# A twelve-layer kernel: the order of work around a recurrent layer that rides inside an FFN pass

## The chip, the core and the metric

The kernel runs on one core of a Trainium2 chip. Five engines work side by side: PE (TensorE, matrix products), DVE (VectorE), ACT (ScalarE), POOL (GpSimd) and SP (SyncE, which only issues transfers here). Each has its own list of instructions, takes them strictly in order, and waits at semaphores for the others. The metric is device time in microseconds; before the change it was 1217.29 us, the median of three runs (1212.4 to 1217.9).

## What is computed

Two sequences of 512 tokens with 256 features pass through twelve layers: four blocks of FFN, token mixing, FFN. The change touches the first block and, of the last one, the preparation of a weight matrix. Cut to that:

```python
def ffn0(x, w_gate, w_up, w_down):                  # 256 -> 1024 -> 256
    return (silu(x @ w_gate.T) * (x @ w_up.T)) @ w_down.T

def rglru(x, W_xy, ig_w, ig_b, ag_w, ag_b, a_param, conv_w, conv_b, W_resid):
    xr, y = split(x @ W_xy.T)                       # 256 features each
    xc = causal_conv1d(xr, conv_w, conv_b)          # 4 taps over time
    gate_x = sigmoid(block_diag(xc, ig_w) + ig_b)
    gate_a = sigmoid(block_diag(xc, ag_w) + ag_b)
    log_a = -8.0 * gate_a * softplus(a_param)
    a = exp(log_a)
    n = xc * gate_x * sqrt(-expm1(2.0 * log_a))
    h = scan(h = a * h + n)                         # over time
    return (gelu(y) * h) @ W_resid.T

def ternary(w):                                     # the last block's FFN weight, 256 x 256
    t = 0.7 * mean(abs(w), axis=-1, keepdims=True)
    return where(w > t, 1, where(w < -t, -1, 0))

x = x + 0.5 * ffn0(layernorm(x))
x = x + rglru(layernorm(x))
x = x + 0.5 * ffn0(layernorm(x))
...                                                 # nine more layers
```

Products are in fp32 precision: each operand is held as a high and a low part (names ending in h and l), and each product is three matmuls (`mm3`, lines 290 to 292).

## The kernel before

**Units.** A unit is one layer for one batch element. Units 0 and 1 are the first FFN for elements 0 and 1, units 2 and 3 the recurrent layer, units 4 and 5 the second FFN. Every engine walks through the units; the code of an engine for a layer is a function such as `pe_ffn`, `act_ffn`, `dve_ffn`. The order inside each of these lists is written out by hand.

**An FFN unit** goes through 8 chunks of 128 hidden features. For chunk j, PE makes gate and up (`gate_up(j)`, 12 matmuls of 512 columns each), ACT the SiLU, DVE the product `ffn_hf`, ACT its high part `ffn_hh` (a rounding copy), DVE the low part `ffn_hl`, and PE the down projection (`down(j)`, 12 matmuls of 256 columns). `chunk(j)` names ACT's or DVE's two steps. SP loads the weights of a chunk into one of two buffers `raw`; POOL splits them into high and low part, gate and up first (lines 522, 525), the down part when the product two chunks back has been used (492, 494). SP loads a chunk when POOL has split the one two back.

**The recurrent layer rides along.** In `RG_OF` unit 1 carries the recurrent layer of element 0 (`r` = 2, `b` = 0), unit 4 that of element 1. Between the chunks PE has the transposes of the normalized x (`pe_T`), the x projection (`pe_rg_x`), the y projection (`pe_rg_y`), the gate products for the two halves of the 256 features (`pe_rg_gates` 0 and 1) and the output projection (`pe_rg_out`). ACT has the convolution's first tap, the high part of its result, the GELU of y, both sigmoids (as Tanh), decay (Exp and Tanh), roots (Sqrt) and the high part of the gated result; DVE has the other taps, the low parts, products, squares, scan, residual and statistics. Projections and gates all write PSUM banks 0 and 1, one after the other; who may write next is told by a semaphore of whoever read last. GELU, SiLU, Exp and Sqrt each want another activation table (Tanh comes with SiLU's and with Exp's), and a change of table is a load on ACT.

**What else is on the lists.** In unit 0, DVE works on sparse positions for a later layer: `d_eq` masks, and in the step behind chunk 7 the rest of a softplus of `a_param` (`dve_softplus_rest`, lines 2685 to 2704) and the places of 2048 entries (2567 to 2574). POOL scatters 16 groups of those entries into a table in HBM, one indirect transfer after the other, each waiting until the one ahead has landed: groups 0 to 5 stand behind the splits of chunks 2 to 7 of unit 1, groups 6 to 9 follow, then comes unit 4's normalization factor (`pool_ln`, line 402); groups 10 to 15 stand in unit 4 in the same way. The four weight blocks of the recurrent layer are split by ACT (`act_rg_weights`) and POOL (`pool_rg_weights`) in unit 0. `dve_ternary` makes the ternary weight: in unit 1 the thresholds, in unit 4 the comparisons. Its matrix `d_q3` is loaded by SP behind the chunks of unit 1 and behind eight stores of zeros (`sp_zero_x`):

```python
            chunks(0)
            chunks(1)
            sp_zero_x(sp)
            sp.dma_start(d_q3[:, :, :], a["weight3"]).then_inc(sem("d_in_q3"), 16)
            chunks(4)
```

`pe_warm` is 12 matmuls whose result nobody reads. They stand ahead of the last down projection of units 1 and 4 and behind the transposes that follow it.

## Time and profile before

| | |
|---|---|
| runs | 1217.29 us median (1212.4, 1217.29, 1217.9) |
| profiled execution | 1215.54 us, its span 1213.3 us |
| PE, DVE, ACT, POOL busy | 91%, 68%, 50%, 45% of the span |
| granted TensorE clock, mean | 0.976 of full speed |
| units 0, 1, 4 | unit 1 begins at 71.96, unit 4 at 139.75, unit 5 at 207.52 us |

In a row of the trace the first number is the start in us from the start of the span, the second the duration in us, then engine, line, operation, written and read tiles, shape; in brackets the idle time of that engine just before, and the engine and line whose work ended it. A line can be that of a helper: lines 290 to 292 are all products, 728 and 732 ACT's two steps of a chunk, 776 and 783 DVE's. Rows of one kind in a row are merged (x4).

### The profile page before, as it was taken

The page shows a single profiled execution, that of the slowest core. Times are in us where ns is not written, and L with a number is a line of the kernel's source. Part 1 is how long each engine was busy: PE and PEld are TensorE (multiplying, and loading weights), DVE is VectorE, ACT ScalarE, POOL GpSimd, SP SyncE. Part 2 cuts the span into 40 slices and gives each one's busy share as a digit, 9 for nine tenths or more (in the row PEclk, how much of TensorE's full clock was granted, in tenths as well). Part 3 has the DMA queues.
Part 4 walks back from the last instruction along what each step waited for, and adds up shares of the span by engine and source line. Part 5 has one row for each costly group of instructions (what it writes and reads, how often), then busy time and mean ns, then how long its engine had stood idle before and what let it go on. Part 6 is the DMA issues. An engine that isn't in the chain of part 4 may idle for free.

```text
span 1213.3 us, 22107 instructions
## 1 busy us (share of the span) xinstructions
PE 1106.9 (91%) x6833; PEld 934.7 (77%) x6833; DVE 827.2 (68%) x2280; ACT 605.2 (50%) x1422; POOL 544.0 (45%) x662
## 2 busy tenths in 40 slices
PE   5988796999899999998989999998899998999997
PEld 4867685777667779966767777996799997899995
DVE  4866657687988865658867876566766665665666
ACT  3436463521112345557747856555455554555552
POOL 6647573751446452235424426324353442444431
PEclk9999997999899999999999999999999999999999
DMA  7215123130004023422102163343011110110101
GB/s 247 89 53 205 29 65 109 57 122 20 1 8 182 1 93 117 136 69 60 34 17 45 43 238 102 117 131 105 28 43 35 43 35 27 37 42 26 52 0 35
DMA packets 48181, 87.81 MB, mean 72 GB/s; under 512 B 9505, under 2 KB 28321, under 8 KB 47521
## 3 DMA queue, kind: packets, MB, share of 16 engines
q1 hardware_dynamic: 41536, 72.98, 19.1%
q0 software_dynamic: 3968, 8.85, 2.5%
q10 hardware_dynamic: 2592, 4.92, 1.2%
q8 instruction: 45, 0.74, 0.3%
q14 instruction: 40, 0.32, 0.1%
HBM read 61.23 MB, written 19.20 MB: 66 GB/s over the span
## 4 chain that ended last, share of the span: by engine, by line
PE 63%; DVE 21%; ACT 8%; issue 4%; DMA 2%; POOL 2%; SPq 1%; DVEq 0%; POOLq 0%; ACTq 0%
PE ps L290 19%; PE ps L292 17%; PE ps L291 17%; DVE a_ptl L1918 4%; PE ps L1894 3%; DVE a_p L1853 2%; ACT a_pth L1910 2%; ACT a_p L1861 2%; PE ps L460 1%; DVE x L1607 1%; PE ps L941 1%; DMA rg_wf<-in_rglru 1%; DVE xl L454 1%; DVE x L1122 1%; PE ps L960 1%
## 5 line engine op out<-in xcount | busy, mean ns | idle before, releaser
L1879 POOL TENSOR_SCALAR a_p<-a_p,small 128x128 f32<-128x128 f32 (+3 forms) x256 | 132.0, 532 | 219.9 <-DVE small L1870 219.8
L1861 ACT ACTIVATE a_p<-a_p,small 128x128 f32<-128x128 f32 (+3 forms) x256 | 141.6, 554 | 77.3 <-DVE small L1853 75.1
L1918 DVE TENSOR_TENSOR a_ptl<-ps,a_pth 128x384 fp32r<-128x384 f32 (+1 forms) x192 | 106.6, 596 | 61.7 <-ACT a_pth L1910 61.5
L290 PE MATMUL ps<-xh,wh 128*128 128x512 f32 x304 | 125.9, 414 | 9.2 <-DVE xl L454 8.1
L291 PE MATMUL ps<-xl,wh 128*128 128x512 f32 x304 | 122.7, 404 | 0.0
L292 PE MATMUL ps<-xh,wl 128*128 128x512 f32 x304 | 122.7, 404 | 0.0
L1910 ACT ACTIVATE a_pth<-ps 128x384 fp32r<-128x384 f32 (+1 forms) x192 | 90.3, 524 | 59.3 <-PE ps L1894 59.2
L1853 DVE CUSTOM_DVE_ANT_0 a_p<-ps,maskrow 128x128 f32<-128x128 f32 (+3 forms) x256 | 111.7, 483 | 4.8 <-PE ps L292 2.1
L402 POOL TENSOR_TENSOR rstd<-veps,nhalf 128x4 f32<-128x4 f32 x24 | 25.9, 1079 | 174.9 <-DVE veps L346 174.9
L494 POOL TENSOR_TENSOR wl<-raw,wh 128x256 fp32r<-128x256 f32 (+1 forms) x64 | 86.2, 1347 | 5.3
L1894 PE MATMUL ps<-ident,a_p 128*128 128x128 f32 x640 | 83.7, 277 | 5.2 <-DVE a_ptl L1918 2.2
L290 PE MATMUL ps<-m_a,xh 128*128 x240 | 83.2, 347 | 5.3 <-DVE xl L1232 2.7
L492 POOL TENSOR_SCALAR wh<-raw 128x256 fp32r<-128x256 f32 (+1 forms) x64 | 46.8, 731 | 80.2 <-PE ps L292 80.1
L1894 PEld LDWEIGHTS ps<-ident,a_p 128*128 128x128 f32 x640 | 71.6, 143 | 8.4 <-DVE a_ptl L1918 2.6
L290 PEld LDWEIGHTS ps<-xh,wh 128*128 128x128 f32 x304 | 59.1, 194 | 24.3 <-DVE xl L454 10.2
L291 PE MATMUL ps<-m_b,xh 128*128 x240 | 72.7, 303 | 0.0
L292 PE MATMUL ps<-m_a,xl 128*128 x240 | 72.5, 302 | 0.0
L292 PEld LDWEIGHTS ps<-xh,wl 128*128 128x128 f32 x304 | 58.7, 193 | 14.5
L1607 DVE SCALAR_TENSOR_TENSOR x<-ps,small,x 128x256 f32<-128x256 f32 x128 | 61.8, 483 | 9.9 <-PE ps L292 3.6
L291 PEld LDWEIGHTS ps<-xl,wh 128*128 128x128 f32 x304 | 59.1, 194 | 11.3
L290 PE MATMUL ps<-drh,xh 128*128 (+2 forms) x160 | 61.7, 385 | 4.0 <-DVE x L1607 4.0
L291 PE MATMUL ps<-drl,xh 128*128 (+2 forms) x160 | 60.3, 377 | 0.0
(366 smaller groups left out, 3352.8 us busy)
## 6 DMA issues: line engine op xcount, KB each, us to landing
raw<-in_w SPq DMA_DIRECT2D x32, 384.0 KB, 3.2
raw<-in_qk SPq DMA_DIRECT2D x16, 512.0 KB, 3.5
raw<-moe_x SPq DMA_DIRECT2D x60, 128.0 KB, 2.3
moe_y<-m_y SPq DMA_DIRECT2D x60, 128.0 KB
m_raw<-in_ex SPq DMA_DIRECT2D x8, 608.0 KB, 7.5
m_a<-in_ex SPq DMA_DIRECT2D x8, 608.0 KB, 5.5
raw<-in_v SPq DMA_DIRECT2D x16, 256.0 KB
moe_x<-drh SPq DMA_DIRECT2D x8, 480.0 KB, 6.1
```

The source lines that it names most:

```text
L290: pe.matmul(o, l[0], r[0], start=start, stop=False, skip_group_check=True)
L291: pe.matmul(o, l[0], r[1], start=False, stop=False, skip_group_check=True)
L292: return pe.matmul(o, l[1], r[0], start=False, stop=stop, skip_group_check=True)
L492: g.tensor_scalar(oh, raw[:, p, at:n], 1.0, 1.0, ALU.mult, ALU.mult).then_inc(sem("w_hi"), 1)
L494: g.tensor_tensor(ol, raw[:, p, at:n], f32(oh), ALU.subtract).then_inc(sem("w_split"), 1)
L1607: v.scalar_tensor_tensor(out=xt, in0=ps[:, 2 + t, e * D:(e + 1) * D], scalar=w_moe1[:, t, 2 * k + e:2 * k + e + 1], in1=xt, op0=ALU.mult, ...
L1853: v.tensor_tensor_reduce(p[:, par, P_AT[i]:P_AT[i + 1]], ps[:, bank, at:at + KEYS[i]], maskrow[:, T - KEYS[i]:T], 1.0, -NEG, ALU.add, ALU.min,
L1861: s.activation(p[:, par, P_AT[i]:P_AT[i + 1]], p[:, par, P_AT[i]:P_AT[i + 1]], ACT.Exp, bias=h_nmx[:, par, i:i + 1], scale=scale, accum_ou ...
L1879: g.tensor_scalar(pp, pp, h_inv[:, par, i:i + 1], 1.0, ALU.mult, ALU.mult).then_inc(sem("at_norm"), 1)
L1894: last = pe.transpose(ps[:, banks[f], at:at + P], p[:, par, P_AT[i] + kb * P:P_AT[i] + (kb + 1) * P], ident[:, :])
L1910: s.activation(dst, ps[:, bank, 0:cols], func, **how).then_inc(sem("at_fhi"), 1)
L1918: ins = v.tensor_tensor(dst, ps[:, bank, 0:cols], f32(hi), ALU.subtract)
```

## The change

PE, ACT and DVE get another order in units 1 and 4; waits are set to match it.

- PE: the gate products move ahead of the y projection and one chunk earlier, the y projection behind `down(4)`, the output projection ahead of `down(5)`.
- ACT: the sigmoids move one chunk earlier, the GELU between roots and gated result, and chunk 5 behind the gated result. Three chunks follow it then, where there were two.
- DVE: the same for its steps; chunk 5 stands ahead of the residual, chunk 6 behind the statistics. Softplus' rest moves from unit 0 to unit 1, behind the low part of the recurrent layer's x; the five place operations (`dve_places`) to the start of unit 1; `dve_ternary` from the end of units 1 and 4 to the place between the first gate product and chunk 4.
- Waits for `const_rgp`, which softplus' rest sets, move from the x projection and the padding to the sigmoids.
- In unit 0 the four weight blocks are copied by ACT behind chunks 0 and 1 (before: two ahead of unit 0, two behind chunk 0) and subtracted by POOL one behind each of chunks 2 to 5 (before: two ahead of chunk 2, then one behind chunks 2 and 3).

```diff
                 gate_up(3)
-                pe_rg_y(pe, r)
+                pe_rg_gates(pe, r, 0)
                 down(2)
                 gate_up(4)
                 down(3)
-                pe_rg_gates(pe, r, 0)
+                pe_rg_gates(pe, r, 1)
                 gate_up(5)
                 down(4)
-                pe_rg_gates(pe, r, 1)
+                pe_rg_y(pe, r)
                 gate_up(6)
+                pe_rg_out(pe, r)
                 down(5)
                 gate_up(7)
-                pe_rg_out(pe, r)
                 down(6)
...
                 act_rg_conv_hi(s, r, 1)
-                act_rg_gelu(s, r)
+                act_rg_sigmoids(s, r, 0)
                 chunk(4)
-                act_rg_sigmoids(s, r, 0)
-                chunk(5)
                 act_rg_sigmoids(s, r, 1)
                 act_rg_decay(s, r)
                 act_rg_roots(s, r)
+                act_rg_gelu(s, r)
                 act_rg_gated_hi(s, r)
+                chunk(5)
                 chunk(6)
                 chunk(7)
...
                     dve_combined(v)
+                    dve_places(v)
                 chunk(0)
                 chunk(1)
                 dve_rg_pad(v, r)
                 dve_T(v, r)
+                if u == 1:
+                    dve_softplus_rest(v)
                 dve_rg_conv(v, r, 0)
                 chunk(2)
                 dve_rg_conv_lo(v, r, 0)
                 dve_rg_conv(v, r, 1)
                 chunk(3)
                 dve_rg_conv_lo(v, r, 1)
+                dve_rg_gate_input(v, r, 0)
+                dve_ternary(v, u)
                 chunk(4)
-                dve_rg_gate_input(v, r, 0)
-                chunk(5)
                 dve_rg_gate_input(v, r, 1)
                 dve_rg_square(v, r, 0)
                 dve_rg_square(v, r, 1)
                 dve_rg_scan(v, r)
                 dve_rg_gated_lo(v, r)
-                chunk(6)
+                chunk(5)
                 dve_residual(v, r, 1.0, [("rg_out", 2 * (r - 2) + 1), ("rg_out", 2 * (r - 2) + 2)], rg_o)
                 dve_stats(v, nxt)
+                chunk(6)
                 chunk(7)
                 dve_residual(v, u, 0.5, ready)
-                dve_ternary(v, u)
                 dve_T(v, nxt)
...
-                    pe.wait_ge(sem("rg_gelu"), DC * b + k + 1)
+                    pe.wait_ge(sem("rg_tap"), DC * b + k + 1)
...
-                pe.wait_ge(sem("rg_tap"), DC * b + c + 1)
+                pe.wait_ge(sem("rg_sigm"), 4 * b + 2 + c + 1)
...
-            if u == 0 and j == 0:
-                act_rg_weights(s, 2)
-                act_rg_weights(s, 3)
+            if u == 0 and j <= 1:
+                act_rg_weights(s, 2 * j)
+                act_rg_weights(s, 2 * j + 1)
...
-            pool_rg_weights(g, 0)
-            pool_rg_weights(g, 1)
             for i in range(1, CH0 // 2):
                 for p in range(2):
                     pool_chunks(g, 0, i, p)
-                    if i == 1:
-                        pool_rg_weights(g, 2 + p)
+                    if i <= 2:
+                        pool_rg_weights(g, 2 * i + p - 2)
```

`dve_places` holds the five operations that stood at lines 2567 to 2574, with the same waits between them.

Three places as they stand on the engines. DVE at the end of unit 0, before (`small` is softplus' data, `d_col` to `d_desti` the places, `xl` the low part of the next unit's x, L477 the residual):

```order
L2703 TENSOR_SCALAR rgp<-rgp 128x2x2
L2704 TENSOR_SCALAR rgp<-small 128x2
L2567 TENSOR_SCALAR d_col<-d_col 128x16
L2568 TENSOR_SCALAR d_col<-d_col 128x16
L2570 TENSOR_TENSOR d_col<-d_col 128x16
L2572 CAST d_small<-d_col 128x16
L2574 CAST d_desti<-d_small 128x16
L454 TENSOR_TENSOR xl<-ps,xh 128x512 x2
L477 SCALAR_TENSOR_TENSOR x<-ps,x 128x256 x4
```

And after, from the last chunk of unit 0 to the first product of unit 1:

```order
L783 TENSOR_TENSOR ffn_hl<-ffn_hf,ffn_hh 128x512
L454 TENSOR_TENSOR xl<-ps,xh 128x512 x2
L477 SCALAR_TENSOR_TENSOR x<-ps,x 128x256 x4
L336 BN_STATS stats<-x 128x6 x4
L342 BN_AGGR mv<-stats 128x2 x4
L345 TENSOR_SCALAR negm<-mv 128x4
L346 TENSOR_SCALAR veps<-mv 128x4
L2536 COPY d_work<-ps 128x128
L2539 TENSOR_TENSOR d_work<-d_work,ps 128x128 x2
L2522 TENSOR_SCALAR d_col<-d_col 128x16
L2523 TENSOR_SCALAR d_col<-d_col 128x16
```

The low part of x follows the last chunk directly, and the places stand ahead of unit 1's first product.

DVE in unit 1 from chunk 3 on, before (`rg_cl` is the low part of the convolution, `rg_xc<-rg_xp,rg_xc` the gate product):

```order
L776 TENSOR_TENSOR ffn_hf<-ffn_s,ps 128x512
L783 TENSOR_TENSOR ffn_hl<-ffn_hf,ffn_hh 128x512
L1505 TENSOR_TENSOR rg_cl<-rg_xc,rg_ch 128x512
L776 TENSOR_TENSOR ffn_hf<-ffn_s,ps 128x512
L783 TENSOR_TENSOR ffn_hl<-ffn_hf,ffn_hh 128x512
L1511 SCALAR_TENSOR_TENSOR rg_xc<-rg_xp,rg_xc 128x512
```

And after (L2616 to L2622 are the ternary thresholds, `d_q` the loaded matrix):

```order
L776 TENSOR_TENSOR ffn_hf<-ffn_s,ps 128x512
L783 TENSOR_TENSOR ffn_hl<-ffn_hf,ffn_hh 128x512
L1510 TENSOR_TENSOR rg_cl<-rg_xc,rg_ch 128x512
L1516 SCALAR_TENSOR_TENSOR rg_xc<-rg_xp,rg_xc 128x512
L2616 TENSOR_SCALAR d_q3n<-d_q 128x512
L2618 TENSOR_TENSOR d_q3t<-d_q,d_q3n 128x512
L2620 TENSOR_REDUCE d_small<-d_q3t 128x2
L2622 TENSOR_SCALAR d_small<-d_small 128x2
L776 TENSOR_TENSOR ffn_hf<-ffn_s,ps 128x512
L783 TENSOR_TENSOR ffn_hl<-ffn_hf,ffn_hh 128x512
L1516 SCALAR_TENSOR_TENSOR rg_xc<-rg_xp,rg_xc 128x512
```

The first gate product and the thresholds stand ahead of chunk 4 now.

ACT behind the roots of unit 1, before (L1478 is the high part of the gated result, L728 with L732 a chunk, L358 the next unit's normalization):

```order
L1472 ACT_TABLE_LOAD
L1472 ACTIVATE rg_ga<-rg_ga 128x512 x2
L1478 ACTIVATE rg_ch<-rg_gy 128x512 x2
L728 ACT_TABLE_LOAD
L728 ACTIVATE ffn_s<-ps 128x512
L732 ACTIVATE ffn_hh<-ffn_hf 128x512
L728 ACTIVATE ffn_s<-ps 128x512
L732 ACTIVATE ffn_hh<-ffn_hf 128x512
L358 ACTIVATE xn<-x,nmr,rstd 128x256 x4
```

And after (L1449 is the GELU):

```order
L1477 ACT_TABLE_LOAD
L1477 ACTIVATE rg_ga<-rg_ga 128x512 x2
L1449 ACT_TABLE_LOAD
L1449 ACTIVATE rg_gy<-ps 128x512 x2
L1483 ACTIVATE rg_ch<-rg_gy 128x512 x2
L728 ACT_TABLE_LOAD
L728 ACTIVATE ffn_s<-ps 128x512
L732 ACTIVATE ffn_hh<-ffn_hf 128x512
L728 ACTIVATE ffn_s<-ps 128x512
L732 ACTIVATE ffn_hh<-ffn_hf 128x512
L728 ACTIVATE ffn_s<-ps 128x512
L732 ACTIVATE ffn_hh<-ffn_hf 128x512
```

The GELU with its table stands behind the roots, and three chunks stand behind the gated result.

## Rows read from the trace of the kernel before

**Rows 1.** The chain that ended last, as shares of the span by engine:

```profile
PE 63%; DVE 21%; ACT 8%; issue 4%; DMA 2%; POOL 2%; SPq 1%; DVEq 0%; POOLq 0%; ACTq 0%
```

**Rows 2.** PE's timeline, units 0 to 5, at the places named:

```profile
23.14 0.39 PE L290 MATMUL ps<-wh,ffn_hh 128*128 128x256 f32 x1 [1.03 <-DVE ffn_hl L783]
...
71.96 0.51 PE L290 MATMUL ps<-xh,wh 128*128 128x512 f32 x1 [2.82 <-DVE xl L454]
...
83.99 0.50 PE L290 MATMUL ps<-xh,rch 128*128 128x512 f32 x1 [1.26 <-DVE xl L454]
...
122.97 0.58 PE L290 MATMUL ps<-rch,rg_ch 128*128 128x256 f32 x1 [6.37 <-DVE rg_cl L1544]
...
132.70 0.39 PE L290 MATMUL ps<-wh,ffn_hh 128*128 128x256 f32 x1 [0.81 <-DVE ffn_hl L783]
...
135.09 1.06 PE L426 MATMUL ps<-ident,xn 128*128 128x128 f32 x8 [0.69 <-issue]
...
139.75 0.50 PE L290 MATMUL ps<-xh,wh 128*128 128x512 f32 x1 [1.00 <-DVE xl L454]
...
150.22 0.49 PE L290 MATMUL ps<-xh,rch 128*128 128x512 f32 x1 [1.42 <-DVE xl L454]
...
189.19 0.58 PE L290 MATMUL ps<-rch,rg_ch 128*128 128x256 f32 x1 [6.37 <-DVE rg_cl L1544]
...
207.52 0.50 PE L290 MATMUL ps<-xh,wh 128*128 128x512 f32 x1 [2.62 <-DVE xl L454]
```

**Rows 3.** DVE's timeline at the end of unit 0 and in unit 1:

```profile
65.78 0.16 DVE L2685 TENSOR_SCALAR small<-small 128x2 f32<-128x2 f32 x1
...
68.75 0.16 DVE L2567 TENSOR_SCALAR d_col<-d_col 128x16 int32<-128x16 int32 x1
...
70.63 1.28 DVE L454 TENSOR_TENSOR xl<-ps,xh 128x512 fp32r<-128x512 f32 x2
...
76.67 0.69 DVE L776 TENSOR_TENSOR ffn_hf<-ffn_s,ps 128x512 f32<-128x512 f32 x1 [0.61 <-PE ps L292]
...
87.16 2.46 DVE L1499 SCALAR_TENSOR_TENSOR rg_xc<-rg_xp,rgp,rg_xc 128x512 f32<-128x512 f32 x3 [3.23 <-ACT rg_xc L1438]
...
98.02 0.69 DVE L1505 TENSOR_TENSOR rg_cl<-rg_xc,rg_ch 128x512 fp32r<-128x512 f32 x1
```

**Rows 4.** SP's timeline in unit 1, the eight stores and the matrix load:

```profile
104.96 6.90 SPq L2409 DMA_DIRECT2D moe_x<-drh  x8
111.90 1.26 SPq L2725 DMA_DIRECT2D d_q<-in_weight  x1
```

**Rows 5.** The view of tile d_q: its load, from issue to landing:

```profile
DMA to landing us min/median/max: 6.9/6.9/6.9
```

**Rows 6.** Windows of DVE's old ternary work (window, length, DVE busy, clock, DMA share, GB/s):

```profile
135.10:138.50 3.40, 3.30 (x6) 1.00 0.33 89
201.90:206.26 4.36, 4.33 (x7) 1.00 0.86 357
```

**Rows 7.** ACT's timeline in unit 1, first second-half sigmoid and second root:

```profile
108.83 0.69 ACT L1455 ACTIVATE rg_xp<-ps,rgp 128x512 f32<-128x512 f32 x1 [0.69 <-PE ps L292]
...
116.73 0.63 ACT L1472 ACTIVATE rg_ga<-rg_ga 128x512 f32<-128x512 f32 x1 [0.32 <-DVE rg_ga L1521]
```

**Rows 8.** POOL's timeline, scatters 6, 8 and 9 and unit 4's normalization:

```profile
121.81 1.33 POOL L2419 DMA_INDIRECT delta_table<-d_work,d_desti  x1 [2.79 <-DMA delta_table<-d_work,d_desti]
...
128.20 0.96 POOL L2419 DMA_INDIRECT delta_table<-d_work,d_desti  x1 [2.71 <-DMA delta_table<-d_work,d_desti]
130.56 0.96 POOL L2419 DMA_INDIRECT delta_table<-d_work,d_desti  x1 [1.40 <-DMA delta_table<-d_work,d_desti]
131.54 1.05 POOL L402 TENSOR_TENSOR rstd<-veps,nhalf 128x4 f32<-128x4 f32 x1
```

**Rows 9.** Windows: length, PE, PEld, DVE, ACT, POOL busy, granted clock, DMA, GB/s:

```profile
123.00:127.80 4.80, 4.80 (x25) 4.80 (x26) 2.04 (x4) 2.20 (x4) 1.10 (x2) 0.58 0.03 5
207.50:214.80 7.30, 7.28 (x25) 5.75 (x26) 3.72 (x12) 2.74 (x3) 3.13 (x4) 0.77 0.11 42
```

More of the change, by code:

```diff
@@ L1420, in pe_rg_out @@
             b = r - 2
+            pe.wait_ge(sem("rg_gelu"), DC * (b + 1))
             pe.wait_ge(sem("rg_glo"), DC * (b + 1))
@@ L1432, in act_rg_x @@
             b = r - 2
-            s.wait_ge(sem("const_rgp"), 2)
+            s.wait_ge(sem("const_in"), 16 * CONSTS)
             s.wait_ge(sem("rg_pad"), b + 1)
@@ L1453, in act_rg_sigmoids @@
             b = r - 2
+            s.wait_ge(sem("const_rgp"), 2)
             s.wait_ge(sem("rg_gates"), 4 * b + 2 * c + 1)
@@ L1484, in dve_rg_pad @@
             b = r - 2
-            v.wait_ge(sem("const_rgp"), 2)
+            v.wait_ge(sem("const_in"), 16 * CONSTS)
             if b == 0:
@@ L2506, in dve_equal, with dve_places, step, settled @@
                     .then_inc(sem("d_eqs"), 1)
+        def dve_places(v):
+            def step(ins):
+                ins.then_inc(sem("d_step"), 1)
+                d_steps[0] += 1
+            def settled():
+                v.wait_ge(sem("d_step"), d_steps[0])
+            step(v.tensor_scalar(d_col[:, 1, :], d_col[:, 0, :], D - 1, 8, ALU.bitwise_and, ALU.logical_shift_left))
+            step(v.tensor_scalar(d_col[:, 2, :], d_col[:, 0, :], 8, None, ALU.logical_shift_right))
+            settled()
+            step(v.tensor_tensor(d_col[:, 3, :], d_col[:, 1, :], d_col[:, 2, :], ALU.bitwise_or))
+            settled()
+            step(v.tensor_copy(d_dest, d_col[:, 3, :]))
+            settled()
+            v.tensor_copy(d_desti[:, :], d_dest).then_inc(sem("d_dest"), 1)
         def dve_combined(v):
@@ L2564, in dve_delta @@
                 v.tensor_scalar(sp_u, sp_y, 1.0, None, ALU.add).then_inc(sem("sp_u"), 1)
-            if u == 0 and j == 7:
-                dve_softplus_rest(v)
-                then(v.tensor_scalar(d_col[:, 1, :], d_col[:, 0, :], D - 1, 8, ALU.bitwise_and, ALU.logical_shift_left))
-                then(v.tensor_scalar(d_col[:, 2, :], d_col[:, 0, :], 8, None, ALU.logical_shift_right))
-                settled()
-                then(v.tensor_tensor(d_col[:, 3, :], d_col[:, 1, :], d_col[:, 2, :], ALU.bitwise_or))
-                settled()
-                then(v.tensor_copy(d_dest, d_col[:, 3, :]))
-                settled()
-                v.tensor_copy(d_desti[:, :], d_dest).then_inc(sem("d_dest"), 1)
             if u == 5 and j == 5:
@@ L2833, in _ @@
             act_T(s, 0)
-            act_rg_weights(s, 0)
-            act_rg_weights(s, 1)
             for u in range(stop):
```

## The prediction

> **What bounds the kernel now.** The chain that ended last comes first: 63% of it is TensorE (PE), 21% DVE [rows 1]. So TensorE's time counts, and an edit pays or costs only where TensorE waits. The change lies in units 0, 1 and 4: three FFN passes, of which unit 1 carries the recurrent layer of batch element 0 and unit 4 that of element 1. TensorE's rows there show where it waits, all for DVE: 2.82 us ahead of unit 1, 6.37 us ahead of each recurrent output projection, 1.00 us ahead of unit 4, 2.62 us ahead of unit 5 [rows 2]. Below, a time in a recurrent unit counts from that unit's x projection, 83.99 in unit 1 and 150.22 in unit 4. From there to the next unit's first matmul it was 139.75 - 83.99 = 55.8 us and 207.52 - 150.22 = 57.3 us; the output projection began at 39.0 in both (122.97, 189.19).
>
> From 83.99 to 122.97 - 6.37 = 116.60 TensorE never pauses and issues 108 matmuls of 512 columns and 60 of 256, worth 138 of 512: 32.61 / 138 = 0.236 us each. So a gate/up pair (12) is 2.83 us, a down projection 1.42, the two gates of one half 1.42, the y projection 2.83, the 12 warm-up matmuls 2.8.
>
> **Start (term A: -0.5).** Two recurrent weight copies leave ScalarE ahead of its first SiLU. TensorE's 1.03 us wait at 23.14 [rows 2] is the most that this gives back. Their two POOL subtracts don't vanish: one stands now behind each of four weight chunks, so later chunks are split later, and TensorE follows those. I take half, -0.5, between -1.0 and +0.6.
>
> **Softplus' rest and the places (term B: -1.3).** From 65.78 to 70.63 DVE worked on both while the transposed x waited [rows 3]. That x needs only ScalarE's copy, so DVE's subtract moves up some 2.7 us and nearly all of the 2.82 us wait goes. But the next link is DVE's product at 76.67, which had waited 0.61 us for TensorE, and the five place operations (68.75 to 70.63, 1.9 us) stand right ahead of it now: -2.7 + 1.9 - 0.6 = -1.4, taken as -1.3 since TensorE pauses longer there. Bounds: -2.3 (places take 1 us when POOL is still), -0.5 (TensorE comes back at its low clock). Softplus' rest (65.78 to 68.75, 3.0 us) goes behind the subtract of the recurrent layer's x, where DVE sat idle 3.23 us for ScalarE [rows 3]; it costs nothing as long as that cover holds, and up to 3.0 if it doesn't.
>
> **Unit 1 (term C: +25.3).** Two things get queued behind something late.
>
> First, the ternary work. Its first DVE step waits for the 256 KB weight matrix, whose load stays where it was in SP's queue: behind unit 1's last chunk and eight zero stores. It was issued at 111.90 [rows 4] and took 6.9 us to land [rows 5]: at 118.8, or 34.8 in unit time. The old place of the work, 135.1, was later than that; the new one is not. SP gets past unit 1's last chunk (stores from 104.96) when POOL has split chunk 5, and that follows down(3), which the new order reaches without the y projection and with one pair of gates ahead: 2.83 - 1.42 = 1.4 us earlier. So the matrix lands at 33.4. DVE is there after the second convolution half (98.02 + 0.69 - 83.99 = 14.7 [rows 3]) and one gate product of that size: at 15.4. It waits 18 us, and behind the waiting instruction stand chunk(4), the second gate product, squares and scan. ScalarE (second-half sigmoids behind chunk(4)) waits for DVE, TensorE stops at down(4), POOL at chunk 6. The work took 3.4 us with POOL beside it [rows 6]; with POOL stopped I take 2.6. DVE is free at 36.0.
>
> From there the path is the old one, entered one chunk earlier: chunk(4)'s product and copy, 1.3 us, then second-half sigmoids to output projection as before, 122.97 - 108.83 = 14.1 us, less 0.3 for the wait ahead of the second root [rows 7]. The GELU now between root and gated copy has room under DVE's scan, since ScalarE had nothing there. Output projection at 36.0 + 15.1 = 51.0, where it was 39.0: **+12.0**. The table load that each unit saves earns nothing, ScalarE being the one that waits.
>
> Second, what follows the projection. Three chunks stand behind it instead of two. A down projection whose product is queued behind residual and statistics started 132.70 - 122.97 = 9.7 us after it [rows 2]; that is down(6) now, then come warm-up, down(7), transposes: 9.7 + 1.4 + 2.8 + 1.4 = 15.3 us. With transposes (1.0) and warm-up the next unit could start 19.1 us after the projection (before: 16.8). But POOL is later still. Its split of chunk 7 needs down(5), which follows the projection now (4.8 + 1.4 us), so it ends at +7.8. Behind it in POOL's queue stand scatters 5 to 9, each waiting for the one ahead to land, and only then unit 4's normalization. Undisturbed steps took (130.56 - 121.81) / 3 = 2.92 us, the last issue 1.0 [rows 8]: normalization at 7.8 + 4 x 2.92 + 1.0 = +20.5, transposes 135.09 - 131.54 = 3.55 us later, at +24.0. Before, the scatters ran beside the scan and were done in time. TensorE has paused 7 us by then. After its 6.37 us pause it ran 4.8 us at a granted clock of 0.58 [rows 9], a mix of 1.2 and 2.4 GHz; so transposes and warm-up, 3.8 us at full clock, take 4.8 + (3.8 - 0.58 x 4.8) = 5.8, about 6. Next unit at +30.0, not +16.8: **+13.3**. Sum +25.3. Bounds: ternary 1.9 to 3.4; a scatter step 2.36 to 3.67, the shortest and longest undisturbed one (-2.2 to +3.0); transposes and warm-up 3.8 to 7.6.
>
> The Trainium skill, "DMA: Bandwidth & Descriptors", section Anatomy of one DMA, fits a POOL-queue DMA with about 2.0 us plus bytes over 436 GB/s. By that (an estimate) a scatter of 4 KB would step at 2.0 and not 2.92, and the sum would be 3.7 us less. The rows decide here.
>
> **Unit 4 (term D: -5.7).** Nothing is loaded here. Ternary's second half is arithmetic, 4.3 us with POOL beside it [rows 6]; I take 3.3 (1.9 to 4.3). From 15.4 that frees DVE at 18.7; + 15.1 puts the output projection at 33.9, not 39.0: -5.1. Behind it 19.1 us, not 207.52 - 189.19 = 18.3: +0.8. POOL has one scatter there, so it is in time. Ternary no longer stands ahead of unit 5's x: the 2.62 us wait goes, and the low clock behind it: the 24 matmuls that follow took 7.3 us at a granted 0.77 [rows 9], at 0.236 they take 5.7, and I count -1.4.
>
> **Sum.** -0.5 - 1.3 + 25.3 - 5.7 = +17.8. The profiled execution took 1215.5 us (span 1213.3), 0.14% under the median of the runs, 1217.29. 1215.5 + 17.8 = 1233.3, say **1233**.
>
> **Rivals.**
> (1) Faster: the transfers are hidden. With the matrix there at 15.4, 18 us sooner, and scatters under 0.7 us apart, DVE is free at 18.0, the projection starts at 33.0, the next unit at 52.1, not 55.8: -3.7, in all -11.2: 1204.3. For it: unit 4 will look so. Against: nothing moved in SP's queue [rows 4]. 0.04.
> (2) Matrix in time, scatters not: 33.0 + 30.0 = 63.0, +7.2, in all -0.3: 1215.2. 0.03.
> (3) Matrix late, scatters hidden: 51.0 + 19.1 = 70.1, +14.3, in all +6.8: 1222.3. For it: before, they ended in time for the transposes [rows 2, 8]. Against: five landings don't fit into 3 us. 0.08.
>
> **Chances.** The forecast has 0.85. Faster by over 0.5% (6 us, about what a measurement of this kernel can tell from no change): rival 1, 0.04. Within: rival 2 and half of rival 3, 0.07. Slower: 0.89. The bounds of the terms, seldom all at one end, give 1225 to 1240; the rivals, 0.15, stay outside.
>
> **What would show it.** Right: in unit 1 a first ternary row on DVE behind some 18 us of idle time that the weight load ends; TensorE idle some 17 us ahead of down(4); five scatters between unit 1's last split and unit 4's normalization on POOL, and TensorE's transposes behind that; no wait over 1 us ahead of units 1 and 5; unit 4's output projection near 34. Wrong: a ternary row within 1 us of the gate product (rivals 1, 2), or transposes some 15 us behind the projection (rival 3).

## The result and the profile after

The changed kernel took 1235.91 us (median of 4 runs, 1234.34 to 1238.6) against 1217.6 us (4 runs, 1212.4 to 1223.2): ratio 1.0158, 95% interval 1.0127 to 1.019. That is 18.3 us slower. The prediction was 1233.0, with a range of 1225 to 1240. The profiled execution took 1236.6 us, its span 1234.1.

The chain that ended last looks as it did [rows 1]; shares over the whole span don't show a change of 1.6%:

```profile
PE 62%; DVE 21%; ACT 8%; issue 5%; POOL 2%; DMA 1%; SPq 1%; DVEq 0%; POOLq 0%; ACTq 0%
```

PE's timeline of the changed kernel, at the places that answer to [rows 2] (start, length, operation, and in brackets the idle time ahead and what ended it):

```profile
24.85 0.50 PE L290 MATMUL ps<-xh,wh 128*128 128x512 f32 x1 [0.83 <-POOL wl L525]
...
67.51 0.50 PE L290 MATMUL ps<-xh,wh 128*128 128x512 f32 x1
...
80.05 0.68 PE L290 MATMUL ps<-xh,rch 128*128 128x512 f32 x1
...
117.96 0.58 PE L290 MATMUL ps<-wh,ffn_hh 128*128 128x256 f32 x1 [16.03 <-DVE ffn_hl L783]
...
131.96 0.55 PE L290 MATMUL ps<-rch,rg_ch 128*128 128x256 f32 x1 [5.16 <-DVE rg_cl L1549]
...
154.81 1.94 PE L426 MATMUL ps<-ident,xn 128*128 128x128 f32 x8 [7.80 <-issue]
...
160.15 0.58 PE L290 MATMUL ps<-xh,wh 128*128 128x512 f32 x1
...
206.85 0.55 PE L290 MATMUL ps<-rch,rg_ch 128*128 128x256 f32 x1 [6.47 <-DVE rg_cl L1549]
...
225.14 0.58 PE L290 MATMUL ps<-xh,wh 128*128 128x512 f32 x1
```

The waits ahead of units 1, 4 and 5 are gone, and two new ones stand in unit 1: 16.03 us ahead of down(4), and 7.80 us ahead of unit 4's transposes. The second is put down to "issue", PE's own queue; POOL's and ACT's rows below show whom it waited for.

DVE's timeline of the changed kernel shows the first one, from the gate product to chunk 4:

```profile
96.55 1.10 DVE L1516 SCALAR_TENSOR_TENSOR rg_xc<-rg_xp,rg_xc 128x512 f32<-128x512 f32 x1
113.81 0.43 DVE L2616 TENSOR_SCALAR d_q3n<-d_q 128x512 f32<-128x512 f32 x1 [16.16 <-DMA d_q<-in_weight]
...
115.83 0.69 DVE L776 TENSOR_TENSOR ffn_hf<-ffn_s,ps 128x512 f32<-128x512 f32 x1
```

And SP's timeline says why the matrix came then: the load still stands behind the zero stores, as in [rows 4]:

```profile
100.72 8.19 SPq L2414 DMA_DIRECT2D moe_x<-drh  x8
108.95 1.19 SPq L2738 DMA_DIRECT2D d_q<-in_weight  x1
```

It landed 4.8 us after its issue, by the view of tile d_q (6.9 before [rows 5]):

```profile
DMA to landing us min/median/max: 4.8/4.8/4.8
```

POOL's timeline of the changed kernel shows the second wait: the down split of chunk 7, five scatters, unit 4's normalization (to compare with [rows 8]).

```profile
137.95 0.41 POOL L492 TENSOR_SCALAR wh<-raw 128x256 fp32r<-128x256 f32 x1 [11.51 <-PE ps L292]
...
139.33 1.06 POOL L2424 DMA_INDIRECT delta_table<-d_work,d_desti  x1 [0.16 <-issue]
143.23 0.96 POOL L2424 DMA_INDIRECT delta_table<-d_work,d_desti  x1 [2.84 <-DMA delta_table<-d_work,d_desti]
145.58 0.96 POOL L2424 DMA_INDIRECT delta_table<-d_work,d_desti  x1 [1.39 <-DMA delta_table<-d_work,d_desti]
147.93 0.96 POOL L2424 DMA_INDIRECT delta_table<-d_work,d_desti  x1 [1.40 <-DMA delta_table<-d_work,d_desti]
150.28 0.96 POOL L2424 DMA_INDIRECT delta_table<-d_work,d_desti  x1 [1.39 <-DMA delta_table<-d_work,d_desti]
151.27 1.05 POOL L402 TENSOR_TENSOR rstd<-veps,nhalf 128x4 f32<-128x4 f32 x1
```

ACT's timeline: the normalization of x that the transposes need, idle until POOL was done:

```profile
152.64 2.07 ACT L358 ACTIVATE xn<-x,nmr,rstd 128x256 f32<-128x256 f32 x4 [10.13 <-POOL nmr L406]
```

All runs can be laid side by side by the starts of four stages on PE, as above. x1 and x4 are the recurrent x projections of units 1 and 4, R1 and R4 the output projections, U4 and U5 the first matmuls of the next units; "rest" is from U5 to the end of the span. Times in us, one profile each:

| kernel | x1 | x1 to R1 | R1 to U4 | U4 to x4 | x4 to R4 | R4 to U5 | rest |
|---|---|---|---|---|---|---|---|
| before | 83.99 | 38.98 | 16.78 | 10.47 | 38.97 | 18.33 | 1005.8 |
| before again (e10) | 82.56 | 38.96 | 17.21 | 10.48 | 39.01 | 17.48 | 1007.4 |
| after | 80.05 | 51.91 | 28.19 | 10.56 | 36.14 | 18.29 | 1009.0 |
| after again (e6) | 81.22 | 51.76 | 30.12 | 10.58 | 36.18 | 18.57 | 1009.2 |
| e1 early load | 80.61 | 36.86 | 29.46 | 10.56 | 36.16 | 18.45 | 1009.3 |
| e2 ternary at ends | 82.94 | 34.60 | 28.16 | 10.56 | 34.46 | 20.19 | 1006.0 |
| e3 scatters in gap | 81.25 | 51.74 | 19.56 | 10.57 | 36.14 | 18.93 | 1008.6 |
| e4 e1 and e3 | 79.93 | 36.65 | 18.51 | 10.58 | 36.18 | 18.08 | 1006.1 |
| e5 e3, ternary behind chunk 7 | 81.23 | 34.44 | 19.80 | 10.56 | 34.47 | 20.19 | 1008.1 |
| e7 before, ternary moved alone | 82.88 | 52.71 | 15.82 | 10.55 | 40.02 | 15.16 | 1008.6 |
| e8 before, new start alone | 79.64 | 39.29 | 17.04 | 10.48 | 39.01 | 17.87 | 1011.9 |
| e9 e3, ternary in unit 4's holes | 80.49 | 34.43 | 19.62 | 10.56 | 34.47 | 18.08 | 1006.2 |

### The profile page after: what moved, and what is told of

It is laid out like the page before. It is cut to its first block, busy times and chain, and to the rows that moved or that the text cites. A ratio compares the mean times of both kernels' runs of the same rounds, so it can differ in the third digit from the quotient of the medians.

```text
span 1234.1 us, 22111 instructions
## 1 busy us (share of the span) xinstructions
PE 1113.2 (90%) x6833; PEld 940.0 (76%) x6833; DVE 827.4 (67%) x2280; ACT 602.4 (49%) x1420; POOL 542.8 (44%) x662
## 4 chain that ended last, share of the span: by engine, by line
PE 62%; DVE 21%; ACT 8%; issue 5%; POOL 2%; DMA 1%; SPq 1%; DVEq 0%; POOLq 0%; ACTq 0%
PE ps L290 18%; PE ps L291 16%; PE ps L292 16%; DVE a_ptl L1923 4%; PE ps L1899 3%; PE ps L460 2%; DVE a_p L1858 2%; ACT a_pth L1915 2%; ACT a_p L1866 1%; DVE x L1612 1%; PE ps L426 1%; PE ps L944 1%; DVE stats L336 1%; DVE x L1125 1%; PE ps L963 1%
## 5 line engine op out<-in xcount | busy, mean ns | idle before, releaser
L732 ACT ACTIVATE ffn_hh<-ffn_hf 128x512 fp32r<-128x512 f32 x32 | 20.2, 632 | 89.8 <-DVE ffn_hf L776 89.8
```

## The experiments

The theory, from the prediction: two transfers cost some 25 us, the weight load that DVE waits for in order and the scatters that POOL runs through ahead of unit 4's normalization; the rest of the change gains some 8 us. The main rival: the new order, three chunks behind the tail, is itself what costs. The first four kernels tell these apart, each against runs of the kernel before.

**e1: the load earlier in SP's queue.**

```diff
             chunks(0)
+            sp.dma_start(d_q3[:, :, :], a["weight3"]).then_inc(sem("d_in_q3"), 16)
             chunks(1)
             sp_zero_x(sp)
-            sp.dma_start(d_q3[:, :, :], a["weight3"]).then_inc(sem("d_in_q3"), 16)
```

> The changed kernel with one line moved: SP issues the load of the weight matrix ahead of unit 1's weight chunks instead of behind them and the eight stores of zeros. Theory (DVE's in-order wait of 16.16 us for this load sets the output projection of unit 1): the wait is gone, the first ternary operation follows the gate product at once, the output projection comes about 36 us after the x projection as in unit 4 (now 51.9), and with the scatters still ahead of unit 4's normalization (next unit 28.2 us behind the output projection) the time falls by 15 to 16 us, to about 1220. Rival (the three chunks behind the tail cost the time, the wait only fills a gap that PE would have anyway): under 3 us, about 1234. Rival (something else on the path is nearly as late, a scatter or a weight split): 5 to 10 us.

Measured: 1221.49 us, ratio to the kernel before 1.0028 (1.001 to 1.0047). DVE's timeline of e1, same place as above:

```profile
96.81 1.10 DVE L1516 SCALAR_TENSOR_TENSOR rg_xc<-rg_xp,rg_xc 128x512 f32<-128x512 f32 x1
97.83 0.84 DVE L2616 TENSOR_SCALAR d_q3n<-d_q 128x512 f32<-128x512 f32 x1
```

No wait is left, x1 to R1 falls from 51.9 to 36.9, and the time by 14.4 us. R1 to U4 stays at 29.5: the second cost doesn't depend on the first.

**e2: the ternary work back at the ends of both units.**

```diff
                 dve_rg_gate_input(v, r, 0)
-                dve_ternary(v, u)
                 chunk(4)
...
                 dve_residual(v, u, 0.5, ready)
+                dve_ternary(v, u)
                 dve_T(v, nxt)
```

> The changed kernel with the ternary work alone put back to the ends of units 1 and 4, where the kernel before has it; the load stays where it is. Theory: no 16 us wait, and DVE's tail starts without the ternary work, so unit 1's output projection comes 32 to 34 us after its x projection (now 51.9) and unit 4's 32 to 34 (now 36.1); the scatters keep unit 4's start 28 us behind the output projection; the ternary operations at the ends cost 0 to 3 us in unit 4 and nothing in unit 1, where the scatters are later. About 1216 (1213 to 1220). Rival (the new order of chunks, not the load, makes unit 1 late): 1230 or more.

Measured: 1219.58 us, ratio 1.0009 (0.9988 to 1.003): the upper end of what was expected. Both output projections came as expected (34.6, 34.5). What fell short of 1216 was x1, 82.94 in this profile, and R4 to U5, 20.2 and not 18.3. At the end of unit 4 the ternary work is not free: PE waits for DVE there again, 0.88 us. Another 0.7 us of it stand ahead of down(6), which came 10.1 us behind R4 and 9.4 in after, with the ternary work in neither stretch.

**e3: the scatters in POOL's idle gap.** Groups 5 to 9 are issued inside chunk 7 of unit 1, where POOL stood idle for 11.51 us until down(5) let the down split go.

```diff
-        def pool_chunks(g, u, i, p):
+        def pool_chunks(g, u, i, p, mid=()):
...
+                if mid:
+                    pool_scatter(g, mid)
                 if positive(ring - 1):
                     g.wait_ge(sem("w_used"), ring - 1)
...
-                    pool_chunks(g, 1, i, p)
-                    pool_scatter(g, [2 * i + p - 2])
-            pool_scatter(g, range(6, 10))
+                    last = (i, p) == (CH0 // 2 - 1, 1)
+                    pool_chunks(g, 1, i, p, range(5, 10) if last else ())
+                    if not last:
+                        pool_scatter(g, [2 * i + p - 2])
```

> The changed kernel with scatter groups 5 to 9 issued on POOL inside unit 1, between the gate and up split and the down split of chunk 7, where POOL stood idle for 11.51 us, instead of behind chunk 7 and ahead of unit 4's normalization; the load stays late. Theory (the scatters alone hold unit 4's start 28.2 us behind the output projection): unit 4 starts 18 to 19 us behind the output projection as unit 5 does, the time falls by 9 to 10 us, to about 1226.5; the 16 us wait stays. Rival (the transposes or the last down products bind as well): 0 to 4 us, 1232 to 1236.

Measured: 1225.83 us, ratio 1.0068 (1.0047 to 1.0089), 10.1 us under the changed kernel. POOL's timeline of e3, the last scatter and the normalization:

```profile
137.79 0.96 POOL L2426 DMA_INDIRECT delta_table<-d_work,d_desti  x1 [1.40 <-DMA delta_table<-d_work,d_desti]
140.33 0.40 POOL L492 TENSOR_SCALAR wh<-raw 128x256 fp32r<-128x256 f32 x1 [1.59 <-PE ps L292]
...
141.80 1.05 POOL L402 TENSOR_TENSOR rstd<-veps,nhalf 128x4 f32<-128x4 f32 x1 [0.24 <-DVE veps L346]
```

The last scatter is issued at 137.79, POOL then waits for PE and DVE again, and the transposes follow down(7) without a pause. R1 to U4 is 19.6, the wait for the load stays at 16.00 us.

**e4: both edits**, e1's line and e3's, in the changed kernel.

> Both edits: the load ahead of unit 1's chunks and scatter groups 5 to 9 in POOL's gap before the down split of chunk 7. Theory: the two costs add, so about 1236 - 15.8 - 9.7 = 1210.5, under the kernel before by 5 to 9 us, since the earlier start of unit 1's x projection (3.9 us) and unit 4's shorter tail (4.4 us) are left. Rival (the order itself costs in both units): 1217 or more. Rival (the gap on POOL is filled by the scatters once the wait for the load is gone, and the down split of chunk 7 comes late): 1213 to 1216.

Measured: 1209.45 us, ratio 0.9938 (0.9915 to 0.9961). The two gains add: 14.4 + 10.1 = 24.5 us one by one, 26.5 together. So the two transfers are the cost, and the new order without them is faster than the kernel before. The rival falls.

**e7: does the wait for the load need the new order?** The ternary work alone is moved, in the kernel before.

```diff
                 dve_rg_gate_input(v, r, 0)
+                dve_ternary(v, u)
                 chunk(5)
...
                 dve_residual(v, u, 0.5, ready)
-                dve_ternary(v, u)
                 dve_T(v, nxt)
```

> The kernel before with one edit: the ternary work of units 1 and 4 behind the first gate product of the recurrent layer instead of at the ends; the order of the gates, the y projection and the chunks as before. Theory: the wait for the load costs the old order too. DVE comes to the ternary work at about 105.4, the load lands at 118.8 or a little earlier, DVE is free at about 120.8, and chunk 5, the second gate product and the tail behind it bring the output projection to 133 to 138 instead of 122.97; but chunk 7's split no longer waits for the output projection, so the scatters end before unit 4's normalization needs POOL and cost nothing: +10 to +15 us from unit 1, 0 to +3 from the ternary half in unit 4, about 1231 (1227 to 1236). Rival (the wait needs the new order of chunks to cost): under +5 us, 1222 or less. Rival (the scatters bind here too): 1240 or more.

Measured: 1227.2 us, ratio 1.0089 (1.0056 to 1.0121). DVE's, POOL's and PE's timelines of e7:

```profile
118.68 0.43 DVE L2603 TENSOR_SCALAR d_q3n<-d_q 128x512 f32<-128x512 f32 x1 [14.38 <-DMA d_q<-in_weight]
```

```profile
139.00 0.96 POOL L2419 DMA_INDIRECT delta_table<-d_work,d_desti  x1 [1.67 <-DMA delta_table<-d_work,d_desti]
144.01 1.05 POOL L402 TENSOR_TENSOR rstd<-veps,nhalf 128x4 f32<-128x4 f32 x1 [4.06 <-DVE veps L346]
```

```profile
135.59 0.58 PE L290 MATMUL ps<-rch,rg_ch 128*128 128x256 f32 x1 [6.27 <-DVE rg_cl L1544]
```

In the old order the wait costs 13.7 us up to R1 (52.7 for 39.0) and the scatters nothing: POOL was through and stood idle 4.06 us for DVE's statistics. The first cost belongs to the moved ternary work, the second to the moved chunks. Unit 4 and its end gave back 1.7 us (55.2 from x4 to U5, 56.9 on average before), where 0 to +3 was expected, and R1 to U4 another 1.2 (15.8 for 17.0). Hence 1227, at the low end of the expected range, and not 1231.

**e8 and e10: the start alone, and the kernel before once more.** e8 is the kernel before with only the new places of the weight splits, of softplus' rest, of the five place operations and of the constants' wait; its core:

```diff
-            if u == 0 and j == 0:
-                act_rg_weights(s, 2)
-                act_rg_weights(s, 3)
+            if u == 0 and j <= 1:
+                act_rg_weights(s, 2 * j)
+                act_rg_weights(s, 2 * j + 1)
...
                     dve_combined(v)
+                    dve_places(v)
...
                 dve_T(v, r)
+                if u == 1:
+                    dve_softplus_rest(v)
```

> The kernel before with only the start of the change: the weight splits spread over unit 0, softplus' rest and the places in unit 1, the constants' wait moved; the recurrent units' order as before and the ternary work at their ends. The prediction put this at -1.8 us (1215.5); the x projections of the five traces of the changed code so far stand at 79.9 to 82.9 against 83.99, so -1 to -4, mean -3.0. Theory now: 1214.5 (1213.5 to 1216.5). Rival (the gain is an accident of the one profile before, whose unit 0 was slow): 1217 to 1218, no difference.

> The kernel before once more, for a second profile. Theory (the start edits are worth about 3 us): unit 1's x projection at 82.5 to 84 again (83.99 before, 82.88 in e7 with the same unit 0; 79.6 to 82.9 in the seven traces with the new start), and from unit 5's start to the end 1006 to 1012 us, as the other traces have it. Rival (the start differs by chance alone): an x projection under 81.5.

Measured: e8 1217.15 us, ratio 0.998 (0.9957 to 1.0004); e10 1215.19 us, a single run. By its time e8 lies in the rival's range and outside the theory's. e10 came as its theory had it, with x1 at 82.56 and a rest of 1007.4. The marks and the times say different things. Nine profiles with the new start have x1 at 79.6 to 82.9, mean 80.8; three with the old one at 82.6, 82.9 and 84.0, mean 83.1. That is 2.3 us, with one overlap (e2). In e8's times 1.1 us is left, and its interval holds zero. So the start's gain is read off the marks and not shown by the times: the rest of the program, the same code in all twelve, took 1005.8 to 1011.9, a scatter wider than the effect, and the 1011.9 are those of e8.

**e6: the changed kernel once more.**

> The changed kernel itself once more, for a second profile and more times. By marks in the traces the first profile started unit 5 17.6 us later than the kernel before and made 1.5 us of that good at once, yet ended 20.8 us later, with stretches of half clock around 358 and 1044 us that the profile before has shorter or not at all. Theory (these stretches scatter between executions): the difference at unit 5's start is again 16 to 18 us, and other or no half-clock stretches follow; time 1233 to 1238. Rival (the change shifts later work into half clock for good): the same stretches stand at the same places, and the difference at the end is 20 us or more again.

Measured: 1237.37 us, ratio 1.0157 (1.0124 to 1.019). U5 stood at 225.14 and 228.43 in the two profiles of after, at 207.52 and 205.70 in those of before: 20.2 us apart on average, over the 16 to 18 that the theory had. The rest was 1009.0 and 1009.2, 1 us over the mean of all twelve profiles. The stretch of half clock near the end came again, and the two spans end 24.3 us apart (1237.6 and 1213.3), as the rival has it. But the kernel before has the stretch too, in e10. Windows of after and of e10 (window, length, PE, PEld, DVE, ACT, POOL busy, granted clock, DMA share, GB/s):

```profile
1033.00:1039.00 6.00, 5.23 (x21) 4.54 (x20) 1.71 (x3) 1.58 (x3) 4.22 (x3) 0.50 0.33 97
```

```profile
1010.00:1017.00 7.00, 6.23 (x28) 5.54 (x28) 1.71 (x3) 1.58 (x3) 4.97 (x4) 0.54 0.25 84
```

e3, which keeps the 16 us wait, has no such stretch (granted clock 1.00 from 990 to 1050). Of the twelve profiles seven have it, four with the new order (after, e6, e1, e5) and three with the old (e10, e7, e8). Their rest is 1009.1 us on average, that of the other five 1006.5. So it comes and goes with either kernel, goes with some 2.5 us, and isn't what the change costs.

**e5 and e9: a better place for the ternary work.** With the scatters in the gap, the ternary work costs 1.7 to 2.2 us of each tail (x to R 36.2 to 36.7 with it, 34.5 without). e5 puts both halves behind chunk 7, ahead of the last residual.

```diff
                 dve_rg_gate_input(v, r, 0)
-                dve_ternary(v, u)
                 chunk(4)
...
                 chunk(7)
+                dve_ternary(v, u)
                 dve_residual(v, u, 0.5, ready)
```

> The changed kernel with scatter groups 5 to 9 in POOL's gap (as in e3) and the ternary work of both units behind chunk 7 and ahead of the last residual, where DVE stood idle for 2.8 to 3.1 us waiting for PE; the load stays in its late place. Theory: the load has landed by then, DVE's tail starts without the ternary work, so output projections come 34.5 us behind the x projections in both units (e2 showed 34.6 and 34.5; e4 has 36.7 and 36.2), next units 18.5 us behind them: 3.7 us under e4, about 1205.7 (1203 to 1208). Rival (the ternary work, 2.0 and 2.3 to 4.3 us there, spills over the hole and delays the residual or the transposed operand): 1208 to 1211.

Measured: 1208.36 us, ratio 0.9922 (0.9895 to 0.9949). The time lies in the rival's range, just over the theory's. The tails came as expected, the ends didn't: R1 to U4 19.8 and R4 to U5 20.2, against 18.5 and 18.1 in e4. About half of that is PE's clock: from output projection to the next down projection, the same matmuls, it took 5.26 us in both units of e5, 4.44 and 4.24 in e4. Windows of unit 1 in e5 and in e4 (granted clock 0.50 and 0.62):

```profile
115.67:120.93 5.26, 5.26 (x24) 5.26 (x25) 2.04 (x4) 2.15 (x4) 1.56 (x2) 0.50 0.09 32
```

```profile
116.58:121.02 4.44, 4.44 (x25) 4.44 (x26) 2.05 (x4) 2.14 (x4) 1.64 (x2) 0.62 0.03 6
```

In unit 4 the edit doesn't set this: e9, whose output projection there follows the same idle time (5.42 us), took 4.24 us at 0.65. In unit 1 ACT's timeline of e5 shows POOL late again, since the projection comes 2 us earlier and the five scatters don't:

```profile
129.98 2.08 ACT L358 ACTIVATE xn<-x,nmr,rstd 128x256 f32<-128x256 f32 x4 [2.82 <-POOL nmr L406]
```

The ternary work itself fits its hole in unit 1, where DVE still waits 0.43 us for PE behind it. In unit 4 it spills over, as the rival has it: PE waits 0.35 us for DVE ahead of U5. e9 moves both halves into unit 4, where e4 showed DVE idle for 2.12 us ahead of chunk 0 and for 3.22 us ahead of the convolution.

```diff
                     dve_places(v)
+                else:
+                    dve_ternary(v, 1)
                 chunk(0)
...
                     dve_softplus_rest(v)
+                else:
+                    dve_ternary(v, 4)
                 dve_rg_conv(v, r, 0)
```

> The changed kernel with scatter groups 5 to 9 in POOL's gap (as in e3), and both ternary halves in unit 4, in two holes that the traces of e4 show on DVE: the first half (2.0 us) ahead of chunk 0, where DVE stood idle for 2.12 us, the second (2.3 us) behind the transposed operand and ahead of the convolution, where it stood idle for 3.22 us. Theory: both tails start without ternary work (output projections 34.6 us behind the x projections), nothing stands at the ends (next units 18.5 and 18.1 us behind them), and unit 4's x projection stays 10.6 us behind its start: x projection of unit 1 to the start of unit 5 in 116.2 us (before 123.5, e4 120.0, e5 119.5), about 1205.5 (1203 to 1208). Rival (the first half is later than the hole allows and moves chunk 0 of unit 4, as it spilled over in e5): 118 to 120 us on that stretch, 1207 to 1210.

Measured: 1207.07 us, ratio 0.9922 (0.99 to 0.9944). DVE's timeline of e9, both halves and what follows each:

```profile
135.59 0.42 DVE L2621 TENSOR_SCALAR d_q3n<-d_q 128x512 f32<-128x512 f32 x1
...
137.78 0.69 DVE L778 TENSOR_TENSOR ffn_hf<-ffn_s,ps 128x512 f32<-128x512 f32 x1
...
144.96 0.34 DVE L2631 TENSOR_SCALAR d_q<-d_q,d_small 128x256 f32<-128x256 f32 x1
...
147.15 1.74 DVE L2634 TENSOR_TENSOR d_q3t<-d_q,d_q3n 128x512 f32<-128x512 f32 x1
148.81 2.31 DVE L1509 SCALAR_TENSOR_TENSOR rg_xc<-rg_xp,rgp,rg_xc 128x512 f32<-128x512 f32 x3
```

U4 to x4 stays at 10.56, so the first half is hidden whole, and x4 to R4 at 34.47, so the second is too. x1 to U5 is 117.2 us, expected 116.2, before 123.5. R1 to U4, 19.6 and not 18.5, is what fell short. About half is again the low clock behind the output projection (5.26 us at 0.50 to 4.44 at 0.62, of which 0.6 is left at down(6), after a shorter wait for DVE). The other half stands ahead of the transposes, where ACT waits 2.63 us for POOL as in e5. e4, e5 and e9 are all faster than both kernels; their intervals overlap, and e9 has the lowest median.

## Why the prediction was right

It foresaw the sign, the size, both mechanisms and their place. Step by step, with the averages of the two profiles of each kernel where there are two:

**Start and places (terms A and B), -1.8 predicted, -2.3 by the marks of all twelve profiles, -2.6 by these four.** In the first pair of profiles it looked like -3.94; more profiles brought it back. The 1.03 us wait at the first down projection (0.59 in e10) went. The 0.83 us that PE waits for POOL's split at 24.85, which is what the prediction halved the term for, stand in the first profile of after alone: in e6 and e8, with the same start, PE goes on there without a pause. The places took 1.2 us and not 1.9 (71.52 to 72.76), near the bound for a still POOL, but in e10 they took 1.4 at their old place. The cover for softplus' rest held, with 0.51 us of idle time left ahead of the convolution. How the gain splits between A and B no run shows.

**Unit 1 (term C), +25.3 predicted, +25.0 measured.** x1 to U4 was 80.10 and 81.88, before 55.76 and 56.17. The output projection came 12.9 us later, predicted 12.0, and what follows it took 12.2 us more, predicted 13.3. That these two misses cancel is luck. Inside the term:

- The matrix landed at 33.7 us of unit time, predicted 33.4. Two errors cancelled: the issue came at 28.9, not 26.5, behind stores that began 1.1 us later and took 8.19 us and not 6.90, and the landing took 4.8, not 6.9. From the first store to the landing it was 13.0 us, and 13.8 before.
- DVE came to the ternary work at 17.6 and not 15.4 (96.55 + 1.10 - 80.05). The wait was 16.2 instead of 18. This cost nothing, the load being last.
- The ternary work took 2.0 us, not 2.6; DVE was free at 35.8, predicted 36.0.
- From there to the output projection it took 16.1 us, not 15.1 (14.9 in e7), so R1 is 51.9 and not 51.0. The rows name the operation. After and e7 run the same two products behind the second root:

```profile
124.56 2.44 DVE L1533 TENSOR_TENSOR rg_xc<-rg_xc,rg_ga 128x512 f32<-128x512 f32 x2 [0.69 <-ACT rg_ga L1477]
```

```profile
129.42 1.29 DVE L1528 TENSOR_TENSOR rg_xc<-rg_xc,rg_ga 128x512 f32<-128x512 f32 x2 [0.69 <-ACT rg_ga L1472]
```

In after, POOL's timeline has chunk 7's split at that time; in e7 POOL was between two scatters:

```profile
124.83 1.62 POOL L525 TENSOR_TENSOR wl<-raw,wh 128x512 fp32r<-128x512 f32 x1
```

The pair ends at 127.00, 0.55 us behind POOL's 126.45, about the time of one of the two products. POOL's operation took 1.62 us here, and 1.27 at 153.26, when DVE stood idle. The Trainium skill ("SBUF — State Buffer", section SBUF: two separate sides) says that a VectorE operation with two SBUF inputs and a GpSimd operation that reads SBUF exclude each other for a whole instruction. These rows agree: the pair took 1.15 us more in after than in e7.

- Normalization at R1 + 19.3, predicted 20.5: the steps between undisturbed scatters were 2.35 us, the lower bound, not 2.92. The first step, 3.90 us, took some of that back. It is the step from scatter 5 to 6, which the sum had left out: 4.36 us in the profile before (from 117.45 to 121.81). The fit of the Trainium skill ("DMA: Bandwidth & Descriptors", section Anatomy of one DMA) that the prediction weighed gives about 2.0 us, an estimate, for such a transfer. The measured 2.35 differs from it, and decides. It lies between that figure and the row that the sum took, and 2.36 stood already in [rows 8], between the last two scatters.
- Transposes to U4 took 5.34 us, predicted 6. e4, where PE doesn't pause ahead of them, has 3.27. The granted clock in these windows, of after and of e4:

```profile
154.81:160.15 5.34, 5.34 (x20) 3.06 (x21) 3.21 (x12) 1.20 (x2) 3.81 (x7) 0.61 0.29 82
```

```profile
131.82:135.09 3.27, 3.27 (x22) 1.96 (x21) 2.96 (x8) 1.08 (x2) 2.08 (x3) 1.00 0.36 120
```

So 2.1 us of the second cost is the low clock after the pause, as the prediction counted it. e1, e2 and e6, which pause there too (7.7 to 7.9 us), ran the same stretch at a granted clock of 0.53 to 0.62. The prediction's +30.0 compares with 28.2 and 30.1.

**Unit 4 (term D), -5.7 predicted, -2.3 measured** (x4 to U5: 54.43 and 54.75, before 57.30 and 56.49). This is the term that was mis-sized, by 3.4 us, in two steps. The first is worth 2.0 us: up to U5 the prediction had -4.3, the other -1.4 lie behind it. x4 to R4 was 36.1, predicted 33.9: the ternary half took 4.3 us (186.57 to 190.82), the upper bound, with POOL splitting weights beside it, and not 3.3; DVE came to it 0.5 us later, and the tail behind it was longer by 0.9. DVE's timeline of after, the half's first and last operation and the next chunk:

```profile
186.57 0.70 DVE L2626 TENSOR_SCALAR d_q<-d_q,d_small 128x256 f32<-128x256 f32 x1
...
189.71 1.19 DVE L2629 TENSOR_TENSOR d_q3t<-d_q,d_q3n 128x512 f32<-128x512 f32 x1
190.82 0.67 DVE L776 TENSOR_TENSOR ffn_hf<-ffn_s,ps 128x512 f32<-128x512 f32 x1
```

e2 and e9 show what the half itself costs there: R4 at 34.5 without it. The second step is the -1.4 us for unit 5's low clock, which was no property of the kernel before. Windows of e10, the second profile of before, and of after, the same 24 matmuls at unit 5's start:

```profile
205.70:211.53 5.83, 5.83 (x24) 4.42 (x25) 3.69 (x12) 2.55 (x3) 3.11 (x4) 1.00 0.13 50
```

```profile
225.14:231.06 5.92, 5.92 (x27) 4.48 (x25) 3.03 (x10) 2.56 (x3) 3.14 (x4) 1.00 0.15 56
```

Where the profile that the prediction read has 0.77 [rows 9], e10 has full clock, behind a wait of 2.25 us (2.62 in [rows 2]).

**Sum.** -2.6 + 25.0 + 0.1 (U4 to x4) - 2.3 = +20.2 up to U5, by the four profiles; the prediction, without its 1.4 us behind U5, had +19.2. The medians differ by 18.3 and, beside e6, by 19.2, but the spans of the four profiled executions by 22.7, 2.5 of it in the rest. So the stages and the medians agree to some 2 to 4 us and no better. The prediction put its +17.8 on a profiled execution that lay 2 us under the median of the four runs of before. So the hit to within 3 us is partly luck: in the two halves of term C, in term D, which the start's gain made up in part, and in executions that scatter by as much. The middle, two waits of some 12 us each that are made by two different parts of the change, was measured part by part. Rivals 1 and 3, the cases without one or both transfers, are kernels now: e4 came to 1209.5 (rival 1: 1204.3), e3, with the load late and the scatters hidden, to 1225.8 (rival 3: 1222.3), e1, with the load in time and the scatters bound, to 1221.5 (rival 2: 1215.2). Each is 3.5 to 6.3 us over the prediction's figure. Term D's 3.4 and the 2 us by which the profile before lay under its median make about that much, though no run takes the two apart.

## What to carry to other kernels

Before work moves to an earlier place on an in-order engine, look up when its inputs land: the transfer keeps its place in the other queue, and everything behind the work waits with it. Before a group of chunks moves behind a long tail, look at what stands behind the last chunk on each other engine: here five scatters in a row, which in the old order ended just when the next unit's normalization wanted POOL [rows 8], held it up. A stretch of low clock is to be seen in a second profile before it is counted as a gain.

## What the runs showed of the hardware

The load of the same 256 KB took 4.8 to 7.7 us from issue to landing in the ten profiles where it stands directly behind the eight stores (6.9 before, 4.8 after), and 3.1 in e1 and e4, where it is issued in unit 0 with no stores ahead of it. From the first store to the landing it was 13.0 to 14.9 us in all ten, whether SP was held by the stores for 6.9 us or for 8.2: a later issue mostly meant a shorter landing. How much of the difference to 3.1 is due to the stores and how much to the moment, no run shows.

The scatters, 4 KB each, stepped at 2.34 to 2.38 us (0.96 issue, 1.39 wait) at least once in every profile. The first step of a row took 2.5 to 5.2 us, the others up to 3.7.

And the time from unit 5's start on, the same instructions in twelve profiles, scattered by 6 us with stretches of half clock that come and go.
